# Moving two shared units behind the routed loop, and the final sum to ScalarE and VectorE

## Chip, cores, metric

One core of one Trainium2 chip. The metric is the device time of the kernel in microseconds, median of repeated runs.

## What is computed

Two layers on 2048 tokens of width 256 (4 batches of 512), each `x = x + ffn(cond(x))`. Layer 0: a conditioned linear map, then 8 linear experts of which each token takes two. Layer 1:

```
x = x + moe(x @ W_base.T + b_base + lora(x) * 2.0)

h = the argument of moe, width 256; experts of width 352
shared = swiglu(h, sh[0]) + swiglu(h, sh[1])
probs  = softmax(h @ gate_w); w, sel = top_k(probs, 2); w = w / sum(w)
routed = sum over e of Wte[:, e] * swiglu(h, exp[e])
out    = shared + routed
swiglu(h, g, u, d) = (silu(h @ g) * (h @ u)) @ d
```

All of layer 1's values are split into a high and a low half in float16, and each product is three matmuls (high-high, low-high, high-low).

## The kernel before

Five engines run hand-ordered programs, tied by semaphores. Layer 0 and the splitting of layer 1's weights into `w1s` fill the first 146 us or so. What follows is layer 1.

**Shared units.** The two shared experts are taken as one of width 704. For each chunk `c` of 512 tokens (four) there are `ST` = 6 blocks of the width, so 24 units `i = 6c + f`; the sixth block of a chunk is half a block. A unit is `gate_up(i)` on TensorE (12 matmuls of 512 columns, 6 for the half block), a silu on ScalarE (L615), a product on VectorE (L977, `s_prod`), the high half on ScalarE (L625, `s_ahi`) and the low half on VectorE (L985, `s_alo`). Units alternate between two pairs of PSUM banks, so unit `i` waits for the product of unit `i - 2`. `down(c)` multiplies a chunk's six blocks by the down weights (17 matmuls for each of its four tiles of 128 tokens) and waits for the low halves of its units; VectorE's `accumulate(c)` (L1008, `s_acc`) adds the result to `x1`. `EARLY` = 18 units run ahead of the routed loop, `down(0)` after unit 7 and `down(1)` after unit 17, the last unit ahead of the loop; unit 18 runs in the loop's drain, units 19 to 23 after it, `down(2)` after unit 19, and `down(3)` last, in two parts (units 18 to 21, then 22 and 23).

**Routing.** Between these units VectorE works out where each token's two copies go (`between`, L1014): `slot_tokens` after unit 13 (`s_rowid`: rows to fetch), `tile_experts` in units 13 to 15 (`s_idx`: the expert of each tile, table `te`). The 4096 copies fill 36 tiles of 128 slots (`TILES`). 28 of them (`FULL`) belong to one expert each; 8 (`MIXED`) are shared by two experts, 64 slots each.

**The routed loop.** A software pipeline over tiles (`step(s, par)`), two tiles in flight. For a tile: GpSimd fetches its rows by an indirect DMA (L492), TensorE transposes them (L1335), VectorE copies them to `rT` (L1051), TensorE does gate and up (L1087; a mixed tile in pairs of half width, L1098), ScalarE the silu (L638), VectorE the product (L1057), ScalarE the high and VectorE the low half (L643, L1060), TensorE transposes (L1360), VectorE copies to `aT` (L1043, L1045, `s_rcx`), TensorE multiplies down, ScalarE copies to `yb` (L649, `s_ry`), and GpSimd stores the rows to `results` in HBM (L498, `s_put`). In one `step(s)` TensorE does, in this order, the row transposes of tile `s + 2`, down of tile `s - 1`, transposes of tile `s`, and gate and up of tile `s + 2`. TensorE takes each tile's weight address from registers. A mixed tile's second expert is first copied by SP into fixed buffers `own_gu`, `own_dn` (L424, L427). Tiles 0 to 4 are started outside the loop, then TensorE's hardware loop takes 4 steps a turn, 7 turns, with 7 register loads at the head of each turn; the rest is written out (the drain). Mixed tiles are 4, 8, ..., 32, so the gate of a mixed tile is the last work of a turn. VectorE's and ScalarE's own loops take two steps a turn.

**The final sum.** When all stores are done (L430), SP loads `results` for each chunk `c` and each of the two copies `k` (L435, eight transfers of 512 KB, `s_yg[c]` after both of a chunk) into `yg[c]`. For each of the 16 tiles ScalarE scales the first copy by the token's weight `W1` (L662, `SCALED` says after which unit; 4 activations of 256 elements per chunk), GpSimd adds it to `x1` (L513), and VectorE multiplies the second by `W2` and adds it (`combine(t)`, L965). `shares1` (L845 to L855, ten small instructions) makes `W1` and `W2` on VectorE, between the loop and unit 18's product. The last chunk is combined ahead of its `accumulate(3)`, so the end waits for all 16 combines. `out` leaves in eight transfers of two tiles.

## Time and profile before

| | |
|---|---|
| median of 3 runs | 376.63 us (376.57 to 376.74) |
| the profiled execution's own time | 375.33 us |
| its span | 373.5 us (373.46 in the result) |
| mean granted TensorE clock | 0.994 |
| busy: TensorE, its weight loads | 351.6 us (94%), 218.7 us (59%) |
| busy: VectorE, ScalarE, GpSimd | 235.4, 163.8, 148.7 us |
| TensorE's gates and ups of the shared units | 264 matmuls, 59.5 us |
| down of the shared units | 272 matmuls, 30.7 us |
| last TensorE matmul ends, last VectorE instruction ends | 366.5, 370.6 us |

All times inside the execution count from the span's start. PE is TensorE's matmuls, PEld its weight loads, DVE VectorE, ACT ScalarE, POOL GpSimd, SPq the DMA queue of SP. A wait is put down to what was released last; "issue" is time in which an engine waits for nothing that the profile shows.

### The profile page before, as it was taken

The numbers are of one execution on the slowest core, as the hardware profiler recorded it, in microseconds if no ns is written. First come the engines' busy times: TensorE is split into PE (matmuls) and PEld (weight loads), VectorE is DVE, ScalarE is ACT, GpSimd is POOL, SyncE is SP. The second block draws the span as 40 slices with busy tenths as digits, with TensorE's granted clock in tenths as the row PEclk, the third lists the DMA queues.
The fourth block names the chain that finished last, engine by engine and source line by source line (L and its number), as shares of the span: only waits on it lengthen the run. The fifth ranks groups of instructions, "written<-read, shape, count | busy, mean of one in ns | idle before, by whom it ended". The sixth has DMA issues, their size and how long they took to land.

```text
span 373.5 us, 8018 instructions
## 1 busy us (share of the span) xinstructions
PE 351.6 (94%) x2788; PEld 218.7 (59%) x2789; DVE 235.4 (63%) x592; ACT 163.8 (44%) x277; POOL 148.7 (40%) x235
## 2 busy tenths in 40 slices
PE   7998999999999999999999999999999999999892
PEld 2543544455454454556448776777777667767462
DVE  1357999866665655789885554555556445546476
ACT  1045285578457656535541332323333233322460
POOL 3000554674656544000022354555555546421633
PEclk9999999999999999999999999999999999999997
DMA  7985114424443320010013144443453444113942
GB/s 213 379 340 204 38 48 144 149 77 132 151 141 103 119 105 20 3 56 2 0 30 134 55 153 141 145 166 115 144 189 127 147 164 139 56 44 107 329 157 112
DMA packets 22105, 47.42 MB, mean 127 GB/s; under 512 B 3136, under 2 KB 11584, under 8 KB 21952
## 3 DMA queue, kind: packets, MB, share of 16 engines
q1 hardware_dynamic: 17904, 37.63, 29.4%
q0 software_dynamic: 3456, 9.44, 8.0%
q8 instruction: 16, 0.26, 0.3%
q10 hardware_dynamic: 720, 0.02, 0.1%
q14 instruction: 9, 0.07, 0.1%
HBM read 29.25 MB, written 8.91 MB: 102 GB/s over the span
## 4 chain that ended last, share of the span: by engine, by line
PE 74%; DVE 14%; DMA 4%; issue 4%; ACT 2%; SPq 1%; DVEq 0%
PE bank L1087 54%; PE bank L1098 6%; PE bank L1255 4%; PE bank L1360 3%; PE bank L1111 2%; PE bank L1335 2%; DVE x L820 2%; DMA w1s<-results 2%; DVE x L965 2%; DVE prod L977 1%; DMA x<-wc 1%; DVE w0s L690 1%; DVE hs L678 1%; ACT acts L625 1%; PE bank L1171 1%
## 5 line engine op out<-in xcount | busy, mean ns | idle before, releaser
L483 POOL TENSOR_TENSOR w1s<-piece,w1s 128x170 f16<-128x170 f32 x128 | 61.6, 520 | 78.4 <-ACT piece L575 78.4
L1087 PE MATMUL bank<-w0s,hs 128*128 128x512 f16 x384 | 86.2, 379 | 1.3 <-DVE x L820 1.2
L492 POOL DMA_INDIRECT rows<-token_store,row_in x36 | 35.1, 974 | 85.5 <-DVE row_in L937 47.0
L820 DVE SCALAR_TENSOR_TENSOR x<-bank,coef,x 128x256 f32<-128x256 f32 x128 | 54.8, 477 | 19.1 <-PE bank L1087 18.8
L1087 PEld LDWEIGHTS bank<-w0s,hs 128*128 128x128 f16 x384 | 37.0, 98 | 43.9 <-DVE x L820 1.9
L1087 PE MATMUL bank<-hs,w1s 128*128 128x512 f16 x264 | 59.5, 379 | 2.5 <-DVE prod L977 2.3
L1087 PE MATMUL bank<-w1s,rT 128*128 x336 | 54.5, 313 | 0.3 <-DVE rT L1051 0.3
L498 POOL DMA_INDIRECT results<-yb,row_out x36 | 35.6, 989 | 38.4 <-ACT yb L649 38.4
L1087 PEld LDWEIGHTS bank<-hs,w1s 128*128 128x128 f16 x264 | 25.1, 98 | 32.5 <-DVE prod L977 4.8
L643 ACT ACTIVATE ract<-prod 128x352 f16<-128x352 f32 x36 | 17.9, 497 | 59.0 <-DVE prod L1057 40.8
L1087 PEld LDWEIGHTS bank<-w1s,rT 128*128 128x128 f16 x336 | 31.7, 98 | 14.9 <-issue 0.4
L1051 DVE COPY rT<-bank 128x256 f32<-128x256 f32 x34 | 14.4, 425 | 37.2 <-PE bank L1335 36.2
L1087 PE MATMUL bank<-w1s,aT 128*128 (+1 forms) x252 | 32.2, 273 | 0.8 <-DVE aT L1045 0.8
L1060 DVE TENSOR_TENSOR ract<-prod,ract 128x352 f16<-128x352 f32 x36 | 18.9, 525 | 20.2 <-issue 14.1
L1255 PE MATMUL bank<-w1s,acts 128*128 128x256 f16 x272 | 30.7, 273 | 0.3 <-DVE acts L985 0.3
L1255 PEld LDWEIGHTS bank<-w1s,acts 128*128 128x128 f16 x272 | 26.3, 98 | 4.8 <-DVE acts L985 1.0
L638 ACT ACTIVATE sil<-bank 128x352 f32<-128x352 f32 x36 | 16.7, 464 | 26.2 <-PE bank L1087 22.0
L572 ACT ACTIVATE w1s<-piece 128x1360 f16<-128x1360 f32 x16 | 21.3, 1329 | 14.8 <-DMA piece<-w 14.8
L625 ACT ACTIVATE acts<-prod 128x512 f16<-128x512 f32 (+1 forms) x24 | 15.1, 629 | 26.2 <-DVE prod L977 26.2
L1087 PEld LDWEIGHTS bank<-w1s,aT 128*128 128x128 f16 (+1 forms) x252 | 23.0, 98 | 4.5 <-issue 0.9
L985 DVE TENSOR_TENSOR acts<-prod,acts 128x512 f16<-128x512 f32 (+1 forms) x24 | 16.6, 691 | 9.3 <-ACT acts L625 9.1
L575 ACT ACTIVATE piece<-piece 128x1360 f32<-128x1360 f32 x16 | 21.4, 1337 | 0.5
(173 smaller groups left out, 483.2 us busy)
## 6 DMA issues: line engine op xcount, KB each, us to landing
piece<-w SPq DMA_DIRECT2D x16, 680.0 KB, 3.9
xrow<-w1s SPq DMA_DIRECT2D x8, 704.0 KB
xrow<-w1s SPq DMA_DIRECT2D x8, 384.0 KB
w1s<-results SPq DMA_DIRECT2D x6, 512.0 KB, 8.8
x<-wc SPq DMA_DIRECT2D x4, 512.0 KB, 7.1
w1s<-xT SPq DMA_DIRECT2D x4, 512.0 KB, 11.3
w1s<-w SPq DMA_DIRECT2D x4, 512.0 KB, 10.3
token_store<-xrow SPq DMA_DIRECT2D x4, 512.0 KB, 3.1
```

Of the source, the lines that this page charges most:

```text
L483: ins = nc.gpsimd.tensor_tensor(w1s[:, LO, at], piece[:, i % 2, part], w1s[:, HI, at], ALU.subtract)
L492: pool.indirect_dma_start(rows[:, i % 2], None, token_store, bass.IndirectOffsetOnAxis(row_in[:, slot_tile(i):slot_tile(i) + 1], 0)).then_ ...
L498: pool.indirect_dma_start(results, bass.IndirectOffsetOnAxis(row_out[:, slot_tile(i):slot_tile(i) + 1], 0), yb[:, i % 2], None).then_inc(s ...
L572: nc.scalar.activation(w1s[:, HI, i * PIECE:(i + 1) * PIECE], piece[:, i % 2], ACT.Copy, scale=SW).then_inc(sm["s_pchi"], 1)
L575: nc.scalar.activation(piece[:, i % 2], piece[:, i % 2], ACT.Copy, scale=SW).then_inc(sm["s_pcsc"], 1)
L625: nc.scalar.activation(acts[0:M, c % 2, f, HI], prod[0:M, p], ACT.Copy).then_inc(sm["s_ahi"], 1)
L643: nc.scalar.activation(ract[:, q, HI], prod[:, q, 0:F], ACT.Copy).then_inc(sm["s_rhi"], 1)
L820: nc.vector.scalar_tensor_tensor(x1[:, t], bank[(n + a) % 4][:, h * D:(h + 1) * D], coef[:, t, e:e + 1], x1[:, t], ALU.mult, ALU.add).then ...
L1060: nc.vector.tensor_tensor(ract[:, q, LO], prod[:, q, 0:F], ract[:, q, HI], ALU.subtract).then_inc(sm["s_rlo"], 1)
L1087: mm = nc.tensor.matmul(out_ap, l, r, start=(i == 0), stop=(i == len(terms) - 1))
L1098: mm = nc.tensor.matmul(out_ap, l, r, start=(i == 0), stop=(i == len(terms) - 1))
L1255: mm = nc.tensor.matmul(bank[4 + q][:, 0:D], acts[:, c % 2, f, a, q * P:(q + 1) * P], w_dn(b, f), start=(f == 0 and n == 0), stop=(f == ST ...
```

## The change

- `EARLY` becomes 16: units 0 to 15 run ahead of the loop, with `down(1)` after unit 15. Unit 16 is in the loop's drain where unit 18 was, and unit 17 is put one step later, ahead of the down product of the last tile. Units 18 to 23 follow the loop, `down(2)` after unit 18. The copy `yb` of the last tile (ScalarE's `step(TILES)`) moves behind the silu of unit 17.
- Mixed tiles are now 2, 6, ..., 30: third of each four. SP's waits, the loop's register names and the table move with them. TensorE's five register loads ahead of the loop stand behind `down(1)`. Mixed tiles' empty slots write to a third block of spare rows.
- `shares1` is cut into four pieces, done after VectorE's steps 31 to 34.
- ScalarE scales both copies (32 activations, not 16), three groups of four tiles after unit 18, then half a group on each side of the high half of units 19 to 23. GpSimd's adds are gone. VectorE adds four tiles at once (`combine(n)`, 1024 elements, 8 of them, not 16 of 256): two after unit 18, one in each of units 19 to 23 between product and low half, one after them.
- `out` leaves in one transfer for each of the first three chunks and one for each of the last four tiles.

```diff
-    EARLY = 3 * ST
-    DOWN = {ST + 1: 0, EARLY - 1: 1, EARLY + 1: 2}
+    EARLY = 3 * ST - 2
+    DOWN = {ST + 1: 0, EARLY - 1: 1, 3 * ST: 2}
-    SCALED = {EARLY + 1: (0, 1), EARLY + 3: (2,), B * ST - 1: (3,)}
+    AHEAD = 3
+    FIRST_SUM = 2
-    DUMMY = 2 * P
+    DUMMY = 3 * P
...
         def mixed(i):
-            return i % CYCLE == 0 and 0 < i < TILES
+            return i % CYCLE == 2 and i < MIXED * CYCLE
...
-                    sp.wait_ge(sm["s_ru"], CYCLE * n + 1)
+                    sp.wait_ge(sm["s_ru"], CYCLE * n - 1)
...
-            for t in range(0, NT, 2):
-                sp.wait_ge(sm["s_acc"], t + 2)
-                sp.wait_ge(sm["s_cmb"], t + 2)
-                sp.dma_start(out[:, t:t + 2], x1[:, t:t + 2]).then_inc(sm["s_out"], 16)
+            for c in range(B - 1):
+                sp.wait_ge(sm["s_acc"], (c + 1) * TPB)
+                sp.wait_ge(sm["s_cmb"], K_TOP * (c + 1))
+                tiles = slice(c * TPB, (c + 1) * TPB)
+                sp.dma_start(out[:, tiles], x1[:, tiles]).then_inc(sm["s_out"], 16)
+            for t in range((B - 1) * TPB, NT):
+                sp.wait_ge(sm["s_acc"], t + 1)
+                sp.dma_start(out[:, t], x1[:, t]).then_inc(sm["s_out"], 16)
...
-                pool.wait_ge(sm["s_scaled"], t + 1)
-                nc.gpsimd.tensor_tensor(x1[:, t], x1[:, t], yg[c][:, 0, q], ALU.add).then_inc(sm["s_add1"], 1)
...
+            def scaled(n, part):
+                c, k = n // K_TOP, n % K_TOP
+                act.wait_ge(s_yg[c], 16 * K_TOP)
+                act.wait_ge(sm["s_w1"], 1)
+                for q in part:
+                    t, y = c * TPB + q, yg[c][:, k, q]
+                    nc.scalar.activation(y, y, ACT.Copy, scale=(W1, W2)[k][:, t:t + 1]).then_inc(sm["s_scaled"], 1)
...
                 nc.scalar.activation(sil[0:M, p], gate, ACT.Silu, scale=1.0 / (SH1 * SW)).then_inc(sm["s_sil"], 1)
+                if i == EARLY + 1:
+                    step(TILES, TILES % 2)
+                if i > 3 * ST:
+                    scaled(AHEAD + i - 3 * ST - 1, range(0, TPB // 2))
...
             for i in range(EARLY, B * ST):
                 shared_act(i)
+                if i == 3 * ST:
+                    for n in range(AHEAD):
+                        scaled(n, range(TPB))
+                if i > 3 * ST:
+                    scaled(AHEAD + i - 3 * ST - 1, range(TPB // 2, TPB))
...
-            def combine(t):
-                c, q = t // TPB, t % TPB
-                dve.wait_ge(sm["s_add1"], t + 1)
-                nc.vector.scalar_tensor_tensor(x1[:, t], yg[c][:, 1, q], W2[:, t:t + 1], x1[:, t],
-                                               ALU.mult, ALU.add).then_inc(sm["s_cmb"], 1)
+            def combine(n):
+                c, k = n // K_TOP, n % K_TOP
+                if c < B - 1:
+                    dve.wait_ge(sm["s_acc"], (c + 1) * TPB)
+                if k:
+                    dve.wait_ge(sm["s_cmb"], n)
+                dve.wait_ge(sm["s_scaled"], (n + 1) * TPB)
+                tiles = slice(c * TPB, (c + 1) * TPB)
+                nc.vector.tensor_tensor(x1[:, tiles], x1[:, tiles], yg[c][:, k], ALU.add).then_inc(sm["s_cmb"], 1)
...
-            run_tiles(dve, step, 2)
-            shares1()
+            run_tiles(dve, step, 4, shares1)
+            step(TILES, TILES % 2)
             for i in range(EARLY, B * ST):
-                shared_dve(i)
+                n = FIRST_SUM + i - 3 * ST - 1
+                shared_dve(i, (lambda: combine(n)) if i > 3 * ST else None)
...
             for i in range(EARLY):
                 gate_up(i, TWO - 1 if i == 0 else None)
-                if i == EARLY - 1:
-                    pe.wait_ge(sm["s_idx"], 1)
-                    places = experts(te[0:1, 0:4]) + experts(te[0:1, FULL:FULL + 1])
...
+            pe.wait_ge(sm["s_idx"], 1)
+            places = experts(te[0:1, 0:4]) + experts(te[0:1, FULL:FULL + 1])
             pe.wait_ge(sm["s_acc"], TPB + 1)
...
-                step(j * CYCLE + 3, 1, d0, d3)
-                step(j * CYCLE + 4, 0, d1, g1)
-                step(j * CYCLE + 5, 1, d2, g2, down_own=j * 16 + 16)
-                step(j * CYCLE + 6, 0, d3, g3, gate_own=j * 16 + 32)
+                step(j * CYCLE + 3, 1, d0, d3, down_own=j * 16 + 16)
+                step(j * CYCLE + 4, 0, d1, g1, gate_own=j * 16 + 32)
+                step(j * CYCLE + 5, 1, d2, g2)
+                step(j * CYCLE + 6, 0, d3, g3)
...
                 if s == TILES - 2:
                     gate_up(EARLY)
+                if s == TILES - 1:
+                    pe.wait_ge(sm["s_rprod"], TILES)
+                    gate_up(EARLY + 1)
```

## Rows read from the trace of the kernel before

**Rows 1.** The page, part 1: TensorE, busy us, share of the span, instructions.
```profile
PE 351.6 (94%) x2788; PEld 218.7 (59%) x2789; DVE 235.4 (63%) x592; ACT 163.8 (44%) x277; POOL 148.7 (40%) x235
```

**Rows 2.** Windows: stretch, length, busy us by engine, clock, DMA share, GB/s.
```profile
352.00:367.00 15.00, 12.59 (x90) 8.17 (x87) 11.80 (x19) 8.71 (x19) 9.39 (x12) 1.00 0.49 170
367.00:374.00 7.00, 0.00 (x0) 0.00 (x0) 3.54 (x9) 0.00 (x0) 0.26 (x1) 0.63 0.36 134
```

**Rows 3.** Chain of waits, end of the loop and tail: start us, us, what.
```profile
337.51 0.39 ACT yb L649
...
340.64 0.37 SPq L435
...
343.16 8.06 DMA w1s<-results
...
352.96 0.49 ACT sil L615
```

**Rows 4.** Chain of waits ahead of the loop.
```profile
187.42 9.06 PE bank L1087 x42
```

**Rows 5.** Timeline, loop head: start, length, engine, operation, [idle before, releaser].
```profile
194.96 0.15 DVE L959 COPY te<-te 1x7 int32<-1x7 int32 x1
...
196.20 5.57 PEld L1255 LDWEIGHTS bank<-w1s,acts 128*128 128x128 f16 x51 [0.21 <-issue]
...
208.75 1.96 PE L1087 MATMUL bank<-w1s,rT 128*128 x12 [0.26 <-DVE rT L1051]
```

**Rows 6.** Windows of 2 us at the head of the loop.
```profile
200.00:202.00 2.00, 2.00 (x22) 1.80 (x21) 0.71 (x2) 0.00 (x0) 0.00 (x0) 1.00 0.02 7
```

**Rows 7.** Chain of waits, one turn of the loop.
```profile
229.49 1.91 PE bank L1098 x24
231.40 0.87 issue
...
237.41 1.79 PE bank L1087 x12
```

**Rows 8.** Timeline of the drain.
```profile
322.59 0.28 DVE L1045 COPY aT<-bank 96x128 f32<-96x128 f32 x1
...
323.46 1.15 PE L1087 MATMUL bank<-w1s,aT 128*128 x9
...
336.32 1.16 PE L1087 MATMUL bank<-w1s,aT 128*128 x9 [0.80 <-DVE aT L1045]
...
338.85 0.29 DVE L855 TENSOR_REDUCE st<-t 128x16 f32<-128x128 f32 x1
```

**Rows 9.** Timeline of the tail.
```profile
348.13 1.71 ACT L662 ACTIVATE yg<-yg,st 128x256 f32<-128x256 f32 x4 [5.61 <-DMA yg<-results]
...
359.14 0.57 ACT L615 ACTIVATE sil<-bank 128x512 f32<-128x512 f32 x1
360.02 0.68 DVE L977 SCALAR_TENSOR_TENSOR prod<-bank,sil 128x512 f32<-128x512 f32 x1
360.73 0.63 ACT L625 ACTIVATE acts<-prod 128x512 f16<-128x512 f32 x1 [1.02 <-DVE prod L977]
...
364.11 5.01 DVE L965 SCALAR_TENSOR_TENSOR x<-w1s,st,x 128x256 f32<-128x256 f32 x8
...
364.13 2.36 PE L1255 MATMUL bank<-w1s,acts 128*128 128x256 f16 x20 [0.30 <-DVE acts L985]
369.16 1.42 DVE L1008 SCALAR_TENSOR_TENSOR x<-bank,x 128x256 f32<-128x256 f32 x4
```

**Rows 10.** Groups by line and shape, VectorE: busy, mean ns, idle.
```profile
L1060 DVE TENSOR_TENSOR ract<-prod,ract 128x352 f16<-128x352 f32 x36 | 18.9, 525 | 20.2 <-issue 14.1 <-ACT ract L643 6.2
...
L985 DVE TENSOR_TENSOR acts<-prod,acts 128x512 f16<-128x512 f32 x20 | 13.8, 692 | 7.7 <-ACT acts L625 7.5
```

**Rows 11.** One line, L965: duration ns, least, median and greatest.
```profile
L965 DVE SCALAR_TENSOR_TENSOR x<-w1s,st,x x12: 472/656/953, 355.5 to 368.6; 128x256 f32<-128x256 f32 x12
```

**Rows 12.** DMA issues: KB each, median us from issue to landing.
```profile
out<-x SPq DMA_DIRECT2D x8, 256.0 KB, 2.1
```

More of the change, by code:

```diff
@@ L341, in mixed, with run_tiles @@
         def mixed(i):
-            return i % CYCLE == 0 and 0 < i < TILES
+            return i % CYCLE == 2 and i < MIXED * CYCLE
         def slot_tile(i):
-            return FULL + i // CYCLE - 1 if mixed(i) else i - i // CYCLE
+            return FULL + i // CYCLE if mixed(i) else i - min((i + 1) // CYCLE, MIXED)
         def owner(i):
-            return FULL + 2 * (i // CYCLE - 1) if mixed(i) else slot_tile(i)
+            return FULL + 2 * (i // CYCLE) if mixed(i) else slot_tile(i)
         def landed(i, par):
             return i * 8 + (16 - 8 * par)
-        def run_tiles(eng, step, ahead):
+        def run_tiles(eng, step, ahead, beside=None):
             for s in range(-2, 3):
@@ L364, in run_tiles @@
                 step(j * 2 + 4, 0)
-            for s in range(3 + 2 * pairs, TILES + 1):
+            for s in range(3 + 2 * pairs, TILES):
                 step(s, s % 2)
+                if beside is not None:
+                    beside(s)
         @block.sync
@@ L506, in _ @@
                     put(s - 1)
-            for t in range(NT):
-                c, q = t // TPB, t % TPB
-                if t % TPB == 0 and c != B - 1:
-                    pool.wait_ge(sm["s_acc"], (c + 1) * TPB)
-                pool.wait_ge(sm["s_scaled"], t + 1)
-                nc.gpsimd.tensor_tensor(x1[:, t], x1[:, t], yg[c][:, 0, q], ALU.add).then_inc(sm["s_add1"], 1)
         @block.scalar
@@ L993, in first_rows, with accumulate @@
                                           bank[2 * i][:, 0:D]).then_inc(sm["s_rx"], 1)
-            def accumulate(c, tiles=()):
+            def accumulate(c):
                 if c == B - 1:
-                    dve.wait_ge(sm["s_cmb"], NT)
+                    dve.wait_ge(sm["s_cmb"], B * K_TOP)
                 for q in range(TPB):
@@ L1009, in accumulate @@
                                                    ALU.mult, ALU.add).then_inc(sm["s_acc"], 1)
-                    if tiles:
-                        combine(tiles[q])
             tr_lo(TWO - 1)
```

74 lines of the change are left out of this document (33 added, 41 removed).

## The prediction, made before the changed kernel ran

> **What bounds the kernel now.** I read the busy shares first [rows 1]: TensorE works 94% of the span, so the total changes only where TensorE has gaps or where something other than TensorE sets the end. The windows of the tail show where that is: in the 15 us from 352 to 367 TensorE is busy 12.59 us, and in the 6.5 us after 367 not at all, while VectorE works on [rows 2]. The chain of waits says what holds the tail [rows 3]: the yb copy of tile 35, its store, then the eight loads of the results, a scaling on ScalarE behind which the silu of a shared unit stands until 352.96, and at the very end VectorE's combines. The timeline closes it [rows 9]: TensorE's last matmuls end at 366.49, but eight combines run from 364.11 to 369.12, and only then come the four accumulates, which end at 370.58. So the end is VectorE's, 4.1 us behind TensorE. Where the loads land, and what ScalarE and VectorE do after that, is what counts.
>
> **Sixteen units ahead of the loop.** Units 16 and 17 leave the stretch before the loop. The chain has units 14 to 17 as 42 matmuls in 9.06 us [rows 4], 0.216 each. Unit 16 has 12 matmuls and unit 17 has 6 (its last block is half a block): 18 x 0.216 = 3.9 us by which the loop starts earlier. What the loop needs must then be there earlier. (a) TensorE's five register loads (L1312) move from under unit 17 to behind down(1). In the kernel before, the table of experts was written by 195.11 (194.96 + 0.15) and the next weight load ran at 196.20 [rows 5], so the loads take at most 1.1 us. Behind down(1) they come after 17 queued matmuls of 1.84 us; I charge 0.1, bounds 0 and 1.1. (b) The first mixed tile is now tile 2, not 4. Its own weights are issued once that table is there, and from 200 on the DMA engines are idle (share 0.02) [rows 6], so they have landed. Tile 2's gate stood at 208.75 [rows 5] and comes at 204.8: over 4 us of slack, no charge. The two row fetches wait for nothing new: no charge.
>
> The Trainium skill speaks against the first of these: "Runtime: NRT & Kernel Launch", section "Instruction fetch mechanics", puts a register load at about 200 ns, that is 1.0 us for five if none of it is covered. By that the result below would be 0.9 us later. The row agrees with the size (at most 1.1 us for five); cover is what it can't tell.
>
> **The loop.** Tiles and matmuls are the same; one mixed tile per turn, two steps earlier in the turn. At a turn's boundary TensorE is idle 0.87 us in the typical case, "issue", directly behind a mixed gate [rows 7]: the branch and seven loads. Five of the six boundaries have 0.77 to 0.91. Now an ordinary gate precedes the boundary. If that gate gives the sequencer more lead, the gap shrinks; nothing in the trace says it does, as both gates take nearly the same time (1.91 and 1.79 us [rows 7]). I charge 0, bounds -4.3 (all five closed) and +0.6.
>
> **shares1 in four pieces at steps 31 to 34.** Its ten instructions, some 0.3 us each and the last one done at 339.14 [rows 8], took 3.0 us and hid behind TensorE's unit 19. Now each piece (0.95, 0.8, 0.65, 0.65 us) stands between a tile's low half and the aT copies. At step 31 the aT copies ended at 322.87 and TensorE wanted them at 323.46 [rows 8]: 0.6 us of cover, so the first piece costs 0.95 - 0.6 = 0.35. Once TensorE is later by that, the next steps' cover (0.6 to 0.75, plus 0.35) holds the other pieces. Charge 0.4, bounds 0 and 3.0.
>
> **The drain.** Unit 16 takes unit 18's place at step 34. Unit 17 (6 x 0.216 = 1.3) goes between the last transposes and the last down, where TensorE waited 0.8 us for the aT copies [rows 8]: +0.5. The yb copy of tile 35 now stands behind unit 16's high half and unit 17's silu on ScalarE. Following these one by one, the silu of 17 ends 0.37 us after down(35), where the copy began 0.2 us after it before: +0.15. Behind yb wait GpSimd's last store, and behind that SP's eight loads. Sum for the first of them: -3.9 + 0.1 + 0.4 + 0.5 + 0.15 = -2.7, so 340.64 [rows 3] becomes 337.9. Unit 18 and down(2) need the products of 16 and 17; both are done by 337.0, when unit 18's matmuls (334.5 to 337.1) end. No charge.
>
> **The tail.** The first 1 MB was there for ScalarE at 348.13 [rows 9] and the second at 351.22 (343.16 + 8.06 [rows 3]); now 345.4 and 348.5. ScalarE then scales three groups of four tiles ahead of unit 19's silu. Four scalings take 1.71 us [rows 9], so twelve take 5.1: silu(19) starts at 350.5. From there ScalarE has four scalings per unit: silu 0.57, two scalings 0.86 (the product of 0.68 runs beside them), high half 0.63, two scalings 0.86, sum 2.92 [rows 9], with hand-overs 3.0. TensorE's 12 matmuls (2.6) and VectorE's 0.68 + 1.22 + 0.69 = 2.6 fit under it. 1.22 is the new add of 1024 elements: 512 take 0.692 and 352 take 0.525 [rows 10], so 1.04 ns an element on top. Silu(23) starts at 350.5 + 4 x 3.0 = 362.5; product until 363.8; VectorE's add of n = 6 until 365.0; low half until 365.7; TensorE's last 20 matmuls 2.36 [rows 9] until 368.1; the last accumulate until 368.5. The last add (n = 7, 365.7 to 366.9) is under those matmuls. Before, this was 370.58: -2.1. The span's end lay 2.9 us later, of which a transfer of 256 KB takes 2.1 from issue to landing [rows 12]; now the last one is half as large, and I take 0.3 off (bounds: 0, and half of the 2.1). Total -2.4.
>
> GpSimd's sixteen adds go. A combine took between 472 and 953 ns [rows 11], and the long ones ran while GpSimd was adding. The 1.22 for the new add comes from rows without GpSimd's adds beside them, as it will have none.
>
> **Against the times.** The profiled execution took 375.33, 1.3 below the median of 376.63; its span is 373.46. New span 371.1, own time 373.0, and against the median 376.63 - 2.4 = 374.3. A measurement tells a change from none at about 0.2% here, 0.75 us.
>
> **The rivals.**
> 1. The turn's boundary closes. For it: the gap stands behind the mixed gate in every turn [rows 7]; one of six has almost none, so it can vanish. Against: gates of equal length. Up to 4.3 us less: 370.0 to 373. Chance 0.15.
> 2. ScalarE eats the gain. It has 32 scalings instead of 16, and five units stand behind them instead of four. At 3.5 us per unit (scalings at their own 0.49, plus a hand-over at each wait) the end moves 4 x 0.5 = 2.0 later: 376.3, no change. For it: silu was already held to 352.96 by scalings [rows 3]. Against: scalings follow one another at 0.43. Chance 0.15.
> 3. Slower: TensorE's clock falls in the tail. It was granted in full up to 367, and 0.63 on average past 367 when TensorE had stopped [rows 2]. Now TensorE waits from 349.7 to 351.8 for unit 19's product. If the level fell to 1.2 GHz there and stayed, the last part's 68 matmuls double from 7.3 to 14.7 us, of which about 6.6 reach the end: 380.9. It decides once those matmuls run at half speed for 3.1 us or more. Against: in the 15 us up to 367 TensorE was idle for 2.4 and was granted 1.00 throughout [rows 2]. Chance 0.07.
> 4. The pieces of shares1 are not covered at all: 3.0 instead of 0.4, 376.9, within 0.2%. Chance 0.05.
> 5. The loop's head is late: fetched rows or own weights not there, from +1 to more than 5: 375.5 to 380, mostly slower. Against: over 4 us of slack [rows 5, 6]. Chance 0.08.
>
> **How the numbers follow.** The forecast (373.0 to 375.8, ±1.4 for the period of 3.0 us and for the loads' landing) has 0.50. Faster: 0.50 + 0.15 + a little of 2 = 0.68. Within 0.2%: most of 2 and 4 = 0.17. Slower: 3, most of 5, the rest of 2 = 0.15. Leaving out the lower part of rival 1, rival 3 and part of 5 gives 371.6 to 376.9.
>
> **What would show it.** Units 14 and 15 directly ahead of down(1), and the loop's first gate 3.8 us earlier; no wait on own weights at tile 2's gate. Boundaries near 0.87. A wait of some 0.4 at down(31) and none at 32 to 34. The first result load 2.7 us earlier. In the tail ScalarE without a gap from the first scaling on, silu to silu 3.0 us; the adds 1.22; TensorE idle 2 us ahead of unit 21; the end 2 us behind TensorE's last matmul shrunk to 0.4. The prediction is wrong if the silu period is 3.5 or more, if the boundaries change, or if TensorE waits at the loop's head.

## Result and the profile after

The changed kernel takes 372.05 us (median of 4, 371.08 to 373.18), the kernel before 376.6 beside it (376.39 to 376.74): ratio 0.9895, 95% interval 0.987 to 0.9919. The forecast was 374.3, range 371.6 to 376.9. Run again in two of the sets below, its ratio was 0.993 (0.9905 to 0.9956) and 0.9914 (0.9884 to 0.9944). The mean of the three ratios is 0.9913, a gain of 3.3 us where 2.4 was forecast; the first set alone has 4.55 us, the two later ones 3.1 and 3.0.

The first profile of the changed kernel, page part 1:
```profile
PE 350.8 (95%) x2788; PEld 216.8 (59%) x2789; DVE 234.8 (64%) x584; ACT 168.9 (46%) x293; POOL 135.8 (37%) x220
```
Against [rows 1] TensorE's busy time is the same within a microsecond; GpSimd is 12.9 us less busy, ScalarE 5.1 more. The profiled execution took 371.08 us and its span is 369.3.

Its chain of waits, head, loop and drain (start us, us, what):
```profile
184.81 1.04 PE bank L1311 x32
185.84 5.18 PE bank L1102 x24
191.03 5.57 PE bank L1270 x51
196.59 0.45 PE bank L1249 x8
...
197.04 1.86 PE bank L1270 x17
198.90 3.58 PE bank L1102 x24
...
226.10 1.09 issue
227.19 0.40 PE bank L1347 x4
...
227.60 1.18 PE bank L1113 x18
...
232.56 1.91 PE bank L1113 x24
234.47 0.33 PE bank L1347 x4
...
237.91 0.22 PE bank L1347 x4
...
241.24 0.99 issue
...
315.98 0.38 PE bank L1347 x4
...
326.68 0.12 issue
326.79 1.22 PE bank L1102 x9
...
337.98 0.37 SPq L437
```
L1311 is the 32 matmuls of `inverse`, a small step of the routing in code that the change doesn't touch; they end just where [rows 4] begins. Behind them stand 24 matmuls in 5.18 us instead of 42 in 9.06: the 3.88 us of units 16 and 17, charged at 3.9. down(1) (L1270) ends at 198.90 and the next work, the first gate of the routed tiles, starts at 198.90: there is no gap for the register loads. In the loop the gap "issue" is 1.09 and 0.99 us, not the 0.87 of [rows 7]; the down pair of a mixed tile right behind it (L1113 x18) takes 1.18, and the four row transposes (L1347) that follow the gate of a mixed tile take 0.33 where others take 0.22. The first result load (SPq L437) comes at 337.98 against 340.64 [rows 3].

Its timeline, ScalarE in the tail (start, length, engine, line, operation, tiles, shape, count, idle before and releaser):
```profile
345.26 3.30 ACT L614 ACTIVATE yg<-yg,st 128x256 f32<-128x256 f32 x8 [6.12 <-DMA yg<-results]
348.47 1.69 ACT L614 ACTIVATE w1s<-w1s,st 128x256 f32<-128x256 f32 x4
350.06 0.58 ACT L625 ACTIVATE sil<-bank 128x512 f32<-128x512 f32 x1
350.54 0.89 ACT L614 ACTIVATE w1s<-w1s,st 128x256 f32<-128x256 f32 x2
351.39 0.63 ACT L639 ACTIVATE acts<-prod 128x512 f16<-128x512 f32 x1
351.93 0.89 ACT L614 ACTIVATE w1s<-w1s,st 128x256 f32<-128x256 f32 x2
352.73 0.57 ACT L625 ACTIVATE sil<-bank 128x512 f32<-128x512 f32 x1
...
360.85 0.59 ACT L625 ACTIVATE sil<-bank 64x512 f32<-64x512 f32 x1
```
and the last work of TensorE and VectorE, from the same view:
```profile
364.04 1.23 DVE L986 TENSOR_TENSOR x<-x,w1s 128x1024 f32<-128x1024 f32 x1
364.06 2.36 PE L1270 MATMUL bank<-w1s,acts 128*128 128x256 f16 x20 [0.16 <-DVE acts L1005]
...
365.30 1.58 DVE L1028 SCALAR_TENSOR_TENSOR x<-bank,x 128x256 f32<-128x256 f32 x4
```
ScalarE has hardly a gap from the first scaling on: silu to silu is 2.67 us (350.06 to 352.73). TensorE's last matmuls end at 366.42 and the last accumulate at 366.88, 0.46 behind it; before, the four accumulates stood behind eight combines and ended 4.1 us behind TensorE [rows 9]. TensorE itself did not end earlier: 366.42 here, 366.49 before.

**How two executions are compared.** The head, where nothing is changed, scatters: the matmuls of `inverse` begin at 186.38 in the first profile of before and 184.59 in a second one; in three profiles of the changed kernel at 184.81, 186.41 and 187.61. So times are taken from that start, called A, and the span is cut at events behind it: the loop's end (the row transposes behind its last boundary), the first result load, the first scaling of a result on ScalarE, the end of TensorE's last matmul, and the span's end.

| kernel | A | loop end | first load | first scaling | TensorE's end | scaling to end | A to span's end |
|---|---|---|---|---|---|---|---|
| before, first profile | 186.38 | 133.50 | 154.26 | 161.75 | 180.1 | 25.3 | 187.1 |
| before again | 184.59 | 134.02 | 154.79 | 160.96 | 180.0 | 26.0 | 187.0 |
| changed, first profile | 184.81 | 131.17 | 153.17 | 160.45 | 181.6 | 24.1 | 184.5 |
| changed again | 186.41 | 131.08 | 153.03 | 159.42 | 180.6 | 24.1 | 183.5 |
| changed, third | 187.61 | 131.11 | 153.06 | 159.77 | 180.9 | 24.1 | 183.8 |
| new sum alone | 186.65 | 134.40 | 155.19 | 162.20 | 182.3 | 23.0 | 185.2 |
| old final sum | 187.47 | 131.09 | 153.09 | 159.66 | 181.3 | 27.3 | 187.0 |
| units 16, 17 early | 187.43 | 134.94 | 156.31 | 164.25 | 186.2 | 24.5 | 188.8 |
| mixed tiles fourth | 186.36 | 130.39 | 152.34 | 158.71 | 180.1 | 24.3 | 183.0 |
| shares1 in the tail | 186.66 | 131.09 | 152.44 | 158.83 | 180.0 | 24.1 | 182.9 |
| both of these | 186.60 | 130.19 | 151.60 | 158.16 | 179.4 | 24.2 | 182.3 |
| down(2) after 20, adds between | 184.63 | 131.12 | 153.07 | 159.32 | 178.8 | 22.4 | 181.7 |
| down(2) after 20 | 186.2 | 131.2 | 153.2 | 159.4 | 180.6 | 24.1 | 183.5 |
| all three | 184.77 | 130.05 | 151.48 | 159.47 | 178.5 | 21.9 | 181.4 |

The columns from "loop end" to "TensorE's end" count from A, and so does the last. The changed kernel gains nothing at TensorE's end, which lies 0.5 to 1.6 us later than before. Its whole gain is behind it: from TensorE's last matmul to the span's end it is 2.9 us, where it was 7.0.

### The profile page after: what moved, and what is told of

Its sections match the earlier page's. It is cut to its first block, busy times and chain, and to the rows that moved or that the text cites. A ratio compares the mean times of both kernels' runs of the same rounds, so it can differ in the third digit from the quotient of the medians.

```text
span 369.3 us, 8012 instructions
## 1 busy us (share of the span) xinstructions
PE 350.8 (95%) x2788; PEld 216.8 (59%) x2789; DVE 234.8 (64%) x584; ACT 168.9 (46%) x293; POOL 135.8 (37%) x220
## 4 chain that ended last, share of the span: by engine, by line
PE 74%; DVE 11%; ACT 5%; issue 4%; DMA 4%; SPq 0%; POOL 0%; POOLq 0%; ACTq 0%; DVEq 0%
PE bank L1102 53%; PE bank L1113 7%; PE bank L1270 5%; PE bank L1372 3%; PE bank L1347 3%; DVE x L833 2%; ACT w1s L614 2%; DMA yg<-results 2%; DMA x<-wc 2%; PE bank L1126 1%; ACT sil L625 1%; DVE w0s L703 1%; DVE hs L691 1%; DVE prod L997 1%; PE bank L1186 1%
## 5 line engine op out<-in xcount | busy, mean ns | idle before, releaser
L1270 PE MATMUL bank<-w1s,acts 128*128 128x256 f16 x272 | 30.7, 273 | 0.4 <-DVE acts L1005 0.4
L1270 PEld LDWEIGHTS bank<-w1s,acts 128*128 128x128 f16 x272 | 26.3, 98 | 5.2 <-DVE acts L1005 1.2
L576 ACT ACTIVATE piece<-piece 128x1360 f32<-128x1360 f32 x16 | 21.4, 1337 | 0.5
L997 DVE SCALAR_TENSOR_TENSOR prod<-bank,sil 128x512 f32<-128x512 f32 (+1 forms) x24 | 16.5, 688 | 6.5 <-ACT sil L625 6.3
```

What stands on the lines that cost most here:

```text
L576: nc.scalar.activation(piece[:, i % 2], piece[:, i % 2], ACT.Copy, scale=SW).then_inc(sm["s_pcsc"], 1)
L997: nc.vector.scalar_tensor_tensor(prod[0:M, p], up, SA / (SH1 * SW), sil[0:M, p], ALU.mult, ALU.mult).then_inc(sm["s_prod"], 1)
L1270: mm = nc.tensor.matmul(bank[4 + q][:, 0:D], acts[:, c % 2, f, a, q * P:(q + 1) * P], w_dn(b, f), start=(f == 0 and n == 0), stop=(f == ST ...
```

## The experiments

**The two kernels again.** No edit.

Each experiment is a kernel of its own with the edit shown; its expectation was written before it ran, and its ratio is to the kernel before, run beside it.

> The changed kernel once more, so that the other kernels of this set have a baseline of their own. It also says whether the head, whose code is untouched but which ran 1.57 us earlier in the one changed profile (the 32 matmuls of the inverse start at 184.81 instead of 186.38), is the change's or chance. Theory: chance of the start; the 32 matmuls start anywhere from 184.8 to 186.4 here, and the loop (first gate to the end of the last step) is 1.5 us longer than before whatever the head does. Rival: something in the change makes the head faster; then they start within 0.3 us of 184.8 again.

> The kernel before once more, as a control with a profile of its own: how far two executions of one kernel lie apart, and where. Theory: the head moves by chance (a start of the first matmuls at 6 or at 8 us, a dip of the granted clock between 30 and 60 us), so the 32 matmuls of the inverse start anywhere from 184.8 to 187.5; from them to the end of the span it is 187.1 (as in the first profile of before) within 1 us, the spread being the landing of the result loads (6.4 to 7.9 us after the first one's issue so far). Rival: the stretch behind the inverse is as scattered as the head; then the comparison of stretches is worth little.

> The changed kernel a third time, as the baseline of this set. Theory: the stretch from the inverse's matmuls to the end of the loop is 131.1 us again (131.17 and 131.08 in its two profiles), against 133.5 and 134.0 in the two of the kernel before; from there on the landing of the result loads decides (7.3 us after the first one's issue in one profile, 6.4 in the other), so from the inverse to the span's end 183.5 to 184.5. Rival: the loop's length scatters as well, by half a microsecond or more.

Measured: changed 372.61 (371.43 to 373.36) and 372.68 (370.35 to 373.62); before 375.24, ratio to itself 1.0005 (0.9984 to 1.0027). The head's 1.57 us were chance, as A above shows: in a second profile the kernel before is the earlier one. Two things move in the head, and neither is the change's. The first is how long the first 128 matmuls take. They start at 6.1 to 6.4 us in every profile (the 8 us of the expectation is only where the second part of them begins behind a wait for a load). In nine profiles they end at 13.8; in five, the first of before among them, they end at 14.8 to 15.5, with 17 to 20 matmuls between 6 and 8 us, not 32. Lines of the chain of before's first profile and of the changed kernel's:
```profile
6.31 9.15 PE bank L1111 x128
```
```profile
8.38 5.39 PE bank L1126 x96
```
This is what the first pair of profiles differs in; the profile shows a clock of 1.00 in both, and why they are slow in some was not found. The second is a fall of the granted clock to 0.50, its lower level, from about 32 to 36 us, in eight of the fourteen profiles; TensorE had waited 1.6 us just before, and did so in the others too. Windows of the changed kernel's second profile (columns as in [rows 2]), and of its first:
```profile
30.00:60.00 30.00, 28.59 (x168) 14.01 (x169) 26.00 (x67) 13.23 (x16) 12.45 (x24) 0.94 0.37 115
```
```profile
30.00:60.00 30.00, 28.07 (x172) 14.31 (x172) 27.62 (x70) 14.75 (x19) 12.41 (x24) 1.00 0.42 132
```
A is 184.6 to 184.8 with neither, 186.2 and 186.4 with the slow start alone, 186.4 to 186.7 with the fall alone, and 187.4 to 187.6 with both. The fall shows in the times too: in the third set the changed kernel's executions with a mean clock of 1.00 took 370.35 to 371.75 and those with 0.995 took 372.25 to 373.62. A median depends by up to a microsecond on how many of either it holds.

Behind the head the two profiles of before agree within 0.1 us in all (though its loop differs by 0.5 and its tail by 0.7), the three of the changed kernel within 1.0; that 1.0 is mostly how long the first loads took to land (7.28, 6.39 and 6.71 us from the first one's issue to the first scaling). The stretches can be compared, then, with the landing as their noise. The expected 131.1 for the loop came again in the changed kernel, so there the rival of a scattering loop fell; in the kernel before it holds by half a microsecond.

**Mixed tiles back in the fourth place.**
```diff
-            return i % CYCLE == 2 and i < MIXED * CYCLE
+            return i % CYCLE == 0 and 0 < i < TILES
...
-                step(j * CYCLE + 3, 1, d0, d3, down_own=j * 16 + 16)
-                step(j * CYCLE + 4, 0, d1, g1, gate_own=j * 16 + 32)
-                step(j * CYCLE + 5, 1, d2, g2)
-                step(j * CYCLE + 6, 0, d3, g3)
+                step(j * CYCLE + 3, 1, d0, d3)
+                step(j * CYCLE + 4, 0, d1, g1)
+                step(j * CYCLE + 5, 1, d2, g2, down_own=j * 16 + 16)
+                step(j * CYCLE + 6, 0, d3, g3, gate_own=j * 16 + 32)
```


> The mixed tiles go back to 4, 8, ..., 32, everything else as changed. Theory: the 1.5 us that the loop lost come from the mixed tile that now stands right behind the turn's boundary; with it back ahead of the boundary the boundaries go from 0.99-1.09 to 0.81-0.91, the pair behind each takes 1.10 instead of 1.18 us, and the time falls by 0.9 to 1.5 us against the changed kernel. Rival: the loop's loss has another cause (the loop that starts 3.9 us earlier meets other transfers), and the time stays within 0.3 us. Second rival: the mixed tile's own weights or rows come late in the old place; then the time rises.

Measured: 371.76 (370.79 to 372.55), ratio 0.9911 (0.9886 to 0.9937), 0.85 below the changed kernel of its set, though the intervals overlap. The loop tells more. In the eight profiles of kernels with the mixed tile third it takes 131.06 to 131.2 from A (for the one with 18 units ahead, less their 3.88 us; the one with down(2) behind unit 20 without the adds between is read from the timeline); in the six with it fourth, 129.62 to 130.52, again less 3.88 where 18 units stand ahead. Means 131.1 and 130.15: the third place costs 0.95 us here, 0.5 to 1.6 from pair to pair. The chain of this kernel at a boundary, and at the down pair of a mixed tile:
```profile
225.62 1.91 PE bank L1113 x24
227.53 1.09 issue
228.62 0.39 PE bank L1347 x4
229.01 1.08 PE bank L1102 x9
...
235.56 0.22 PE bank L1347 x4
235.78 1.10 PE bank L1113 x18
```
The size was as expected, its account wasn't. The down pair of a mixed tile does take 1.10 here and not 1.18, but the ordinary down that now stands behind the boundary takes 1.08 and not 0.98: whatever stands there pays. Summed over the chain from A to the loop's end, downs and down pairs with the short gaps at them are 31.2 us in both kernels. What differs is the row transposes: 7.99 us here, 8.93 in the changed kernel. Behind a mixed gate they take 0.33 instead of 0.22, once a turn; with the mixed gate last in the turn, the transposes behind it are those at the boundary, which take 0.39 in either kernel. Why they are slower there was not tested. The gaps are not all shorter: 1.09, 1.07, 0.88, 0.18, 1.04, 0.91 against 1.09, 0.99, 1.00, 0.12, 0.99, 0.99, as long in sum. In the mean of the six profiles with the mixed tile fourth the gaps are some 0.2 us shorter in sum, which is the rest of the 0.95. In before's first profile they were shorter (0.87, 0.91, 0.90, 0.14, 0.81, 0.77). With the mixed gate ahead of it the gap scatters between 0.77 and 1.11, with an ordinary gate there it stays at 0.99 to 1.09. Why was not found. In the kernel with the new sum alone the loop also waited once, some 0.3 us, for a tile's rows to be fetched, which is a part of its 134.40.

**Eighteen units ahead again, with the new final sum.**
```diff
-    EARLY = 3 * ST - 2
-    DOWN = {ST + 1: 0, EARLY - 1: 1, 3 * ST: 2}
+    EARLY = 3 * ST
+    LAST = 19
+    DOWN = {ST + 1: 0, EARLY - 1: 1, LAST: 2}
```
ScalarE's copy `yb` of the last tile goes back ahead of the shared unit too.

> Units 16 and 17 go back ahead of the loop (18 units there), unit 18 stands in the drain, down(2) behind unit 19; loop, final sum and pieces of shares1 as changed. Theory: units ahead of the loop delay the start of the loop by 3.9 us, unit 18 (12 matmuls, 2.6 us) in the drain fills the 0.8 us gap where unit 17 (1.3 us) stands in the changed kernel, so the first result load comes 3.9 + 1.3 = 5.2 us later; the tail then has one shared unit fewer to run behind the loads (two scalings and a half less of ScalarE's chain, some 2.7 us). Net: slower by 2 to 3 us. Rival: TensorE bounds the whole, and moving units between stretches changes nothing (within 0.5 us).

Measured: 375.47 (374.32 to 378.07, 12 executions), ratio 1.0001 (0.9978 to 1.0024): 2.9 slower than the changed kernel of its set. The sum was as expected, its account wasn't. The first load comes 3.2 us later from A than there, not 5.2: unit 18 stands at step 34, where the changed kernel has unit 16, and not in the gap ahead of the last down, so nothing is added in the drain and unit 17 leaves it (3.88 - 0.6 = 3.3). Then something came that the other profiles don't have. Windows of this kernel:
```profile
355.00:366.00 11.00, 7.29 (x22) 2.55 (x21) 7.89 (x9) 9.73 (x23) 0.00 (x0) 0.69 0.59 211
360.00:362.00 2.00, 2.00 (x7) 0.63 (x5) 1.76 (x4) 2.00 (x6) 0.00 (x0) 0.50 0.43 176
```
and its timeline in that stretch:
```profile
359.44 6.75 PE L1102 MATMUL bank<-hs,w1s 128*128 128x512 f16 x18 [3.71 <-DVE prod L997]
```
TensorE had waited 3.71 us for the product of unit 20; the granted clock was 0.69 on average over these 11 us and 0.50, the lower of its two levels, in the middle of them, and 18 matmuls took 6.75 us instead of 3.9. This is the prediction's rival 3, in another kernel: 2.85 us longer for these matmuls, of which 1.5 show at the end (24.5 us from the first scaling, 23.0 in the kernel with the new sum alone, whose tail is the same). Of its 12 executions two have a mean clock of 0.986, as the profiled one, with 377.97 and 378.07; the others have 0.991 or 0.995 and take 374.3 to 376.4. Without those two the median would be about 0.2 us lower, so the 2.9 is not the clock's. The changed kernel's waits at that place (1.63, 0.75 and 1.05 us) left the clock at 1.00, and so did 2.78 us in the profiled execution of the kernel with the new sum alone; another of that kernel's executions, which was not profiled, also has a mean clock of 0.986, with the longest time of its twelve (375.35).

**The old final sum, all else as changed.**
```diff
+            for t in range(NT):
+                c, q = t // TPB, t % TPB
+                if t % TPB == 0 and c != B - 1:
+                    pool.wait_ge(sm["s_acc"], (c + 1) * TPB)
+                pool.wait_ge(sm["s_scaled"], t + 1)
+                nc.gpsimd.tensor_tensor(x1[:, t], x1[:, t], yg[c][:, 0, q], ALU.add).then_inc(sm["s_add1"], 1)
...
-                nc.vector.tensor_tensor(x1[:, tiles], x1[:, tiles], yg[c][:, k], ALU.add).then_inc(sm["s_cmb"], 1)
+                nc.vector.scalar_tensor_tensor(x1[:, t], yg[c][:, 1, q], W2[:, t:t + 1], x1[:, t],
+                                               ALU.mult, ALU.add).then_inc(sm["s_cmb"], 1)
```


> The final sum as in the kernel before: GpSimd adds the first scaled result tile by tile, VectorE scales and adds the second, ScalarE scales only the first; result leaves in pairs of tiles. Shared units, loop and mixed tiles as changed. Theory: the two halves of the change add up; the earlier first load (2.7 us) reaches the end also with the old sum, so the kernel lies 0 to 1.5 us behind the changed one, its end again 3 to 4 us behind TensorE's last matmul. Rival: the new final sum carries the gain; then this kernel is at the time of the kernel before or slower, 3 us or more behind the changed one.

Measured: 375.23 (373.25 to 377.52), ratio 0.9998 (0.9973 to 1.0023). The theory fell and the rival holds: the first load stands where the changed kernel has it (153.09 from A, against 153.17, 153.03 and 153.06), the results are there 1.3 to 2.1 us earlier than before, and nothing of it reaches the end. The timeline of this kernel:
```profile
364.39 0.68 DVE L1003 TENSOR_TENSOR acts<-prod,acts 64x512 f16<-64x512 f32 x1 [0.70 <-ACT acts L640]
365.11 5.02 DVE L983 SCALAR_TENSOR_TENSOR x<-w1s,st,x 128x256 f32<-128x256 f32 x8
370.16 1.42 DVE L1026 SCALAR_TENSOR_TENSOR x<-bank,x 128x256 f32<-128x256 f32 x4
```
The eight combines stand at the end as before [rows 9], and they start 177.6 from A, where before's first profile has 177.7. Five units instead of four stand behind the loads, and their chain takes back what the loads gained. This kernel is not the move of the units alone, though: it also has the mixed tiles in the third place and the pieces of `shares1` in the drain, which cost the changed kernel 0.95 and 0.6 us (above and below). The move of the units with the old sum and without those two was not run.

**The new final sum alone, in the kernel before.**
```diff
-    SCALED = {EARLY + 1: (0, 1), EARLY + 3: (2,), B * ST - 1: (3,)}
+    LAST = EARLY + 1
+    AHEAD = 8 - (B * ST - 1 - LAST)
+    FIRST_SUM = AHEAD - 1
```
with `combine`, `scaled` and the stores of `out` as in the changed kernel; units, mixed tiles and `shares1` as before.

> The kernel before with the new final sum alone: ScalarE scales all 32, VectorE adds four tiles at once in eight adds, GpSimd adds nothing, three quarters of the result leave in one transfer each; 18 units ahead, mixed tiles 4 to 32 and shares1 as before. Theory (formed after the kernel with the old sum came out at the time of before): the end is set by the sum and the units behind the loads; the new sum gives most of the 3 us by itself, 1.5 to 3 us faster than before. Rival, the prediction's own account: the gain is the earlier start of the loads, and ScalarE's 16 more scalings, with the loads landing as late as before, cost as much as they save; then this kernel is within 0.7 us of before.

Measured: 373.77 (373.07 to 375.35), ratio 0.9971 (0.9952 to 0.999), 1.3 us faster than before; from A to the end 1.8 less. So the new sum gives about half by itself, everything else in the change nothing by itself (the kernel above), and together they give 3.1 (from A) to 3.3 (by the ratios): more than the two single gains. The column "scaling to end" shows why. With the old sum it is 25.3 and 26.0 us with four units behind the loads, 27.3 with five; with the new sum 23.0 with four, 24.1 with five. Moving the units costs 1.3 to 2.0 us there with the old sum and 1.0 with the new one, against 1.1 to 1.8 that the first load gains. TensorE's end says it another way. With the new sum alone TensorE waits 2.78 us for the product of unit 21, behind ScalarE's scalings, and ends 2.2 us later than before; the new sum wins 4.1 behind TensorE's end and pays those 2.2. The rest of the change takes back 0.7 to 1.8 of them.

**`shares1` in the tail.**
```diff
-            run_tiles(dve, step, 4, shares1)
+            run_tiles(dve, step, 4)
...
+                if i == 18:
+                    for s in range(TILES - 5, TILES - 1):
+                        shares1(s)
```


> The changed kernel with the ten small operations of shares1 taken out of steps 31 to 34 and put behind unit 18 on VectorE, which waits there for the results anyway. Theory: the waits of TensorE at down(31) and down(32) go (together 0.45 us, the prediction's charge of 0.4), the first result load is 0.4 us earlier, and the time falls by 0.2 to 0.5 us, at the edge of what is measured; in the profile down(31) starts without a wait. Rival: the operations in the tail are late for the first scaling (they take some 3 us from about 340 on, and the results land at 345); then ScalarE waits and the time rises.

Measured: 371.24 (370.87 to 372.5), ratio 0.9896 (0.987 to 0.9922); from A to the first load 0.6 us less, to the end 0.6 to 1.6 less. The first load gains a little more than the expected 0.4. In the times the gain is not told from none: the ratio is 0.6 us below the mean of the changed kernel's, and the intervals overlap.

**Both of these.** The two edits together.

> The changed kernel with two of its parts taken back or moved: mixed tiles 4 to 32, and the operations of shares1 behind unit 18. Theory: the two gains add up, as both shift the first result load; 0.45 to 0.9 us and 0.4 us, so 0.9 to 1.3 us faster than the changed kernel of this set. Rival: from the landing on, ScalarE's or TensorE's chain has slack somewhere and takes no more than one of the two.

Measured: 370.7 (370.15 to 371.51), ratio 0.9877 (0.9844 to 0.991), 2.0 below the changed kernel of its set; from A to the first load 1.5 less, to the end 1.2 to 2.2 less. The two add up. This kernel also says what the moved units are worth beside the new sum, as it differs from the kernel with the new sum alone in little else (the `yb` copy, the place of the register loads, `shares1` behind unit 18 and not ahead of it, down(2) behind unit 18 and not 19): the first load is 3.6 us earlier from A and the end 2.9, 0.3 of it for that kernel's wait in the loop, and the ratios, of different sets, lie 3.5 us apart.

**down(2) behind unit 20.**
```diff
+    LAST = 20
-    DOWN = {ST + 1: 0, EARLY - 1: 1, 3 * ST: 2}
+    DOWN = {ST + 1: 0, EARLY - 1: 1, LAST: 2}
-    AHEAD = 3
+    AHEAD = 8 - (23 - LAST)
```


> The changed kernel with down(2) behind unit 20 instead of 18, so that units 19 and 20 pass ScalarE in its 5 to 6 us of idle time ahead of the landing of the results, and five scalings of four tiles instead of three stand ahead of unit 21. Theory: from the landing on ScalarE sets the end; it then has 20 scalings (8.6 us) ahead of unit 21 and three units at 2.67 us instead of 12 (5.2) and five units: silu(21) comes 8.6 instead of 5.2 + 2 x 2.67 = 10.5 us after the landing, so the end 1.3 to 1.9 us earlier. Rival: TensorE, which has no idle time left there, sets the end, and the gain is below 0.7 us.

Measured: 371.62 (371.05 to 372.74), ratio 0.9906 (0.9879 to 0.9932), 0.3 us below the changed kernel's mean ratio; from A to the end 183.5 (A taken from the timeline), 0 to 1.0 less. Expected were 1.3 to 1.9. The timeline of VectorE and ScalarE in this kernel:
```profile
351.51 2.53 DVE L987 TENSOR_TENSOR x<-x,yg 128x1024 f32<-128x1024 f32 x2
353.96 2.53 DVE L987 TENSOR_TENSOR x<-x,w1s 128x1024 f32<-128x1024 f32 x2
356.41 0.68 DVE L998 SCALAR_TENSOR_TENSOR prod<-bank,sil 128x512 f32<-128x512 f32 x1
```
```profile
353.75 0.60 ACT L626 ACTIVATE sil<-bank 128x512 f32<-128x512 f32 x1
354.25 0.90 ACT L615 ACTIVATE w1s<-w1s,st 128x256 f32<-128x256 f32 x2
357.12 0.63 ACT L640 ACTIVATE acts<-prod 128x512 f16<-128x512 f32 x1 [1.98 <-DVE prod L998]
```
The rival had the size, but not the reason: TensorE was idle for 1.3 us in that stretch (0.84, 0.27 and 0.17), and the next bound was VectorE's order. Its four adds stood behind the accumulates of down(2) and ahead of the product that ScalarE waited for. The kernel before already had its first combines between the accumulates of down(2); the change had given that up.

**The same, with three adds between the accumulates.**
```diff
-            def accumulate(c):
+            def accumulate(c, sums=()):
...
+                    if q - 1 in sums:
+                        combine(q - 1)
```


> The changed kernel with down(2) behind unit 20, and VectorE's first three adds put between the accumulates of down(2) instead of behind them. In the kernel with down(2) behind unit 20 alone, VectorE stood in the accumulates until 351.6 and then did four adds back to back (5.06 us), so the product of unit 21 came 1.98 us late for ScalarE. Theory: the three adds fit in the 1.43 us that VectorE waits ahead of each accumulate, the product of 21 comes 2 us earlier, TensorE's last part ends up to 1.3 us earlier, and the kernel is 0.7 to 1.5 us faster than the changed one. Rival: TensorE has no idle time left from there on (0.84 + 0.27 + 0.17 us in that kernel), so that at most those 1.28 us are to be had, and the accumulates, delayed by the adds, hold back TensorE's down(2); then the gain is below 0.4 us.

Measured: 369.8 (368.15 to 371.33), ratio 0.9854 (0.9818 to 0.9889), 2.9 below the changed kernel of its set; three of its six executions had the clock of 1.00 against three of eleven there, which is some half a microsecond of that. Timeline of VectorE, and of TensorE:
```profile
345.77 0.42 DVE L1029 SCALAR_TENSOR_TENSOR x<-bank,x 128x256 f32<-128x256 f32 x1 [0.67 <-PE bank L1273]
346.11 1.22 DVE L987 TENSOR_TENSOR x<-x,yg 128x1024 f32<-128x1024 f32 x1
347.63 0.42 DVE L1029 SCALAR_TENSOR_TENSOR x<-bank,x 128x256 f32<-128x256 f32 x1 [0.30 <-PE bank L1273]
```
```profile
349.28 6.64 PE L1105 MATMUL bank<-hs,w1s 128*128 128x512 f16 x30
355.76 7.65 PE L1273 MATMUL bank<-w1s,acts 128*128 128x256 f16 x68
```
The adds fit in VectorE's waits, and TensorE runs from 349.28 to 363.41 without a gap: from the scaling on it sets the end, 22.4 us instead of 24.1. From A to the end it is 1.8 to 2.8 us less than in the changed kernel, and 1.8 less than without the adds between: 1.3 of that is TensorE's idle time, as the rival reckoned. Most of the rest is that matmuls split by a wait take longer than the same ones in a row: 5.34 + 1.47 us for the 30 of the last gates and ups in the kernel without the adds between, 6.64 here, and 5.41 + 2.36 against 7.65 for the 68 of down(3).

**All three.**

> All of it: mixed tiles 4 to 32, shares1 behind unit 18, down(2) behind unit 20 with three adds between its accumulates. Theory: 0.9 to 1.3 us of the first two and some of the third's 0.7 to 1.5, so 1.6 to 2.8 us faster than the changed kernel of this set, at 369 to 370.5. Rival: the ten operations of shares1, which now stand in the same stretch of VectorE as the products of units 18 to 20, delay those, and with them down(2); then no faster than the kernel with the first two alone.

Measured: 369.95 (367.71 to 371.28), ratio 0.9853 (0.9814 to 0.9893). No faster than the one before it by its times, as the rival had it (from A 0.3 less). The first load is 1.6 us earlier, but the first scaling is not (159.47 from A against 159.32): the ten operations of `shares1` now hold back the product of unit 19, and ScalarE stands behind it. Timeline of ScalarE:
```profile
341.72 0.63 ACT L640 ACTIVATE acts<-prod 128x512 f16<-128x512 f32 x1 [3.11 <-DVE prod L998]
...
343.71 0.63 ACT L640 ACTIVATE acts<-prod 128x512 f16<-128x512 f32 x1 [0.88 <-DVE prod L998]
344.24 3.29 ACT L615 ACTIVATE yg<-yg,st 128x256 f32<-128x256 f32 x8
```
It and the one before it, at 369.95 and 369.8, have the lowest medians of all; their intervals overlap with that of the kernel with the first two alone.

## Why the prediction was right, and where it was off

The direction and the range held, and so did the picture: the loads' landing and the chains behind it set the end. But the sizes of two parts were off, in opposite directions: the first load came 0.9 to 1.6 us short of its forecast, and the tail behind the first scaling was 1.6 shorter than forecast. That the sum of 2.4 missed by only 0.7 to 0.9 is in part luck, and by one of the prediction's own signs ("if the boundaries change") it was wrong on the loop.

- **Units 16 and 17, 3.9.** 3.88, in each kernel with 16 units ahead. The register loads behind down(1), charged at 0.1, left no gap. The prediction's estimate of 1.0 us for five, from the 200 ns per register of the Trainium skill ("Runtime: NRT & Kernel Launch", section "Instruction fetch mechanics"), is not seen in the result. The Trainium skill gives that figure for registers loaded from HBM, and here the table is in SBUF; the trace can't tell a cheaper load from one covered by the queued matmuls.
- **The loop, 0.** This step failed. It costs 0.95 us in the mean (0.5 to 1.6 from pair to pair), beyond the bound of +0.6. The prediction looked for a gap that closes behind an ordinary gate (rival 1); it got a gap that is never under 0.99 but for one boundary (0.2 us in all over the mean of the kernels with the mixed gate there), and row transposes behind the mixed gate that take 0.11 us more each turn, which makes up the rest. Rival 1 went the other way. The 0.87 that it took as typical was one execution's: before's second profile has 1.11, 0.89, 0.88, 1.01 and 0.88.
- **shares1 0.4, unit 17 0.5, yb 0.15.** In the changed kernel's first profile TensorE is late at down(31) (the down product of tile 31, in the drain), as expected, and also at down(33) (the 0.12 at 326.68 above, and 1.22 for nine matmuls that take 0.98 elsewhere), where nothing was expected. From the loop's end to the first load it is 20.8 us in the three kernels with the drain as before, 21.9 to 22.0 in the seven with unit 17 in it and the pieces in the steps, and 21.4 both with the pieces alone (the kernel with 18 units) and with unit 17 alone (the three with `shares1` in the tail). So the pieces cost 0.6, not 0.4, and unit 17 with yb 0.6, for 0.65. Together with the loop the first load gains 1.1 to 1.8 us from A, not 2.7. The first pair of profiles shows 2.66 and seemed to confirm the 2.7, but 1.57 of it is chance in the head and 1.1 the change.
- **Landing, 7.5 after the first load.** 6.4 to 7.3 in the changed kernel, 6.2 and 7.5 before: no shift that these profiles tell from chance.
- **Silu to silu, 3.0.** 2.67 (2.79 the last): the term of the tail that was mis-sized, 1.2 us over the four units from 350.06 to 360.85. The twelve scalings ahead of them took 4.8 and not 5.1. The prediction added full durations (0.57, 0.86, 0.63, 0.86) and hand-overs on top, but ScalarE's instructions overlap: a silu of 0.58 is followed after 0.48, two scalings of 0.89 after 0.85. The Trainium skill has this: "ScalarE: Activation LUTs", section "What ACT_TABLE_LOAD costs", gives the time of an activation from its length and says that two in a row overlap by about 93 ns. An estimate from that page of the Trainium skill is 2 x 0.52 + 4 x 0.40 = 2.64 (two activations of 512 elements, four of 256 with a scale per partition, each less the overlap), and the trace agrees with 2.67.
- **Adds 1.22, last accumulate 0.4 behind TensorE, last transfer 0.3 less.** 1.22 (1.21 to 1.23); 0.46; the span ends 2.45 us after the last accumulate, not 2.9, so 0.4.
- **Scaling to the span's end.** Expected 25.7 (371.1 - 345.4), measured 24.1: the 1.2 of the period, the 0.3 of the scalings ahead and the 0.1 of the transfer. It makes up for the 0.9 to 1.6 us by which the first load falls short; the landing, up to 1.1 us shorter than the 7.5 forecast, gave the rest by chance.
- **What carries the gain.** The prediction gave it to the moved units (-2.7) and held the new sum to be about neutral (+0.3 in the tail). The runs show that neither does without the other. The new sum alone gives 1.3 us (1.8 from A); all the rest without it gives nothing that can be measured (0.9998), and both give 3.1 to 3.3. With the new sum in place the moved units are worth 2.9 to 3.5, and the third place of the mixed tiles and the pieces of `shares1` take 1.2 to 2.2 of it back. The new sum shortens what follows TensorE's end from 7.0 to 2.9 us, which the prediction had (the combines that no longer stand ahead of the last accumulates).
- **The rivals.** Rival 2 (3.5 us a unit) and rival 5 (the loop's head late) did not come: the first mixed gate stands at 203.30, 3.88 us earlier from A than before. Rival 4 did not either. Rival 3 did not come here, but its mechanism is real, as the kernel with 18 units showed.

## What to carry to other kernels

Cut the span at an event that the change can't touch and compare stretches from there; a difference of whole profiles can agree with a forecast and be chance by half. When one engine is busy 94% of the span, look where its own last work ends: moving its work about can bring that end forward by no more than its idle time, and here the gain lay behind it. A load that lands earlier is worth something only if the chain behind it gets shorter or has room: ask of each half of a change what it gives alone. For an engine that works without a gap, take the distance from start to start, not the durations; and where it is then freed, look at once at the order of work on the next engine, as with VectorE's adds here.

## What the runs showed of the hardware

- A wait of 3.71 us of TensorE was followed by a granted clock of 0.69 over the next 11 us and 6.75 us for 18 matmuls (3.9 at the full level); waits of up to 2.78 us in other profiles were not. Two of 12 executions of that kernel have a mean clock of 0.986, and so has one of the 12 of the kernel with the new sum alone.
- The same code had a granted clock of 1.00 or 0.94 between 30 and 60 us from one profile to the next (eight of fourteen have the fall), with 1.1 to 2.1 us of difference behind it. The first 128 matmuls ended at 13.8 us in nine profiles and at 14.8 to 15.5 in five.
- The landing of the same loads took 6.2 to 7.9 us after the first one's issue.
- One in six loop boundaries has a gap of 0.11 to 0.18 us, always the same one (the fourth), in all thirteen profiles with a chain; the others have 0.77 to 1.11. That was not explained.
- The same nine matmuls of a down product take 1.08 us right behind a loop boundary and 0.98 elsewhere; the pair of a mixed tile 1.18 and 1.10.
- Activations in a row start 0.48 us apart after a silu of 0.58 us, and 0.85 after two scalings that take 0.89 together.
